# Order at the slot seams and both halves of the second MLP product beside the exponentials in a kernel of three transformer layers and a rotation

## The reference, cut to what matters

```
xn = ln(x) * (1 + sc1) + sh1                  # modulation from the condition
q, k, v = split(xn @ w_qkv + b_qkv)           # 16 heads of 18
q, k = ln(q), ln(k)                           # per head, layers 0 and 2 only
o = softmax(q @ k.T * 18**-0.5) @ v
x = x + g1 * (o @ w_proj + b_proj)
h = gelu((ln(x) * (1 + sc2) + sh2) @ w1 + b1) # 288 -> 1152
x = x + g2 * (h @ w2 + b2)                    # the second MLP product
```

## Time and profile before

| | us |
|---|---|
| median of 3 runs (lowest, highest) | 5283.6 (5277.15, 5285.2) |
| the profiled execution: its time | 5279.16 |
| its span in the trace | 5277.4 |
| PE busy | 4467.7 (85%) |
| DVE busy | 3683.8 (70%) |
| ACT busy | 2297.4 (44%) |
| POOL busy | 1110.9 (21%) |
| mean granted TensorE clock | 0.942 of full |

### The profile page before, as it was taken

The page is one execution under the profiler, slowest core; times in us unless marked ns, Lnnn a source line. Parts: engine busy times, 40 slices in busy tenths (PEclk is TensorE's granted clock), DMA queues, the critical chain, the costliest instruction groups (busy, mean ns, idle before and its releaser), DMA issues. The chain is left out here.

```text
span 5277.4 us, 125546 instructions
## 1 busy us (share of the span) xinstructions
PE 4467.7 (85%) x46073; PEld 3701.5 (70%) x46073; DVE 3683.8 (70%) x7723; ACT 2297.4 (44%) x3828; POOL 1110.9 (21%) x2044
## 2 busy tenths in 40 slices
PE   6654888888888886899999999976988989899888
PEld 4543677777777775777777777765777777777776
DVE  5665788777877774666666666656777777777774
ACT  0112445454444543444444444434444444444443
POOL 1001222222222212222222222212122121212121
PEclk7576999999999997999999999997999999999999
DMA  3001010010100001010000100011000000000000
GB/s 69 19 0 47 26 27 27 23 27 21 27 27 24 26 21 55 26 27 25 23 27 27 27 27 27 25 42 31 24 26 19 26 24 21 24 23 26 19 24 17
DMA packets 122230, 141.59 MB, mean 27 GB/s; under 512 B 14446, under 2 KB 117780, under 8 KB 122112
## 3 DMA queue, kind: packets, MB, share of 16 engines
q1 hardware_dynamic: 121968, 139.75, 9.7%
q10 hardware_dynamic: 144, 0.22, 0.0%
HBM read 110.87 MB, written 29.06 MB: 27 GB/s over the span
## 5 line engine op out<-in xcount | busy, mean ns | idle before, releaser
L627 ACT ACTIVATE pT<-S 128x1024 f32<-128x1024 f32 x768 | 745.2, 1022 | 467.5 <-PE S L1134 463.1
L863 DVE TENSOR_REDUCE mx<-S 128x4 f32<-128x1024 f32 x768 | 919.1, 1215 | 26.9 <-PE S L1105 20.0
L575 ACT ACTIVATE hf<-M 128x512 f32<-128x512 f32 (+1 forms) x480 | 266.8, 556 | 927.1 <-PE M L1185 842.7
L922 DVE TENSOR_TENSOR xbo<-M,gM 128x288 f32<-128x288 f32 x192 | 87.8, 457 | 784.1 <-PE M L1224 784.1
L1134 PE MATMUL S<-qT,kT 32*128 32x256 f32 x9216 | 432.2, 298 | 159.3 <-ACT nmT L614 83.7
L504 POOL TENSOR_SCALAR hh<-hf 128x512 fp32r<-128x512 f32 (+1 forms) x480 | 282.7, 589 | 1192.1 <-ACT hf L575 1173.5
L1134 PEld LDWEIGHTS S<-qT,kT 32*128 32x128 f32 x9216 | 336.3, 187 | 240.2 <-ACT pT L627 108.1
L1144 PE MATMUL A<-pT,V 128*32 128x256 f32 x6144 | 415.9, 389 | 19.6 <-ACT pT L627 19.6
L1185 PE MATMUL M<-xh,w_hi 128*128 128x256 f32 x1728 | 388.0, 304 | 4.6 <-POOL xh L480 3.3
L1185 PE MATMUL M<-xl,w_hi 128*128 128x256 f32 x1728 | 347.6, 284 | 40.4 <-DVE xm L786 40.4
L1105 PE MATMUL S<-kT,qT 32*128 32x256 f32 x3072 | 351.2, 337 | 30.9 <-DVE mx L863 24.0
(11 more groups left out here) (229 smaller groups left out, 10190.6 us busy)
## 6 DMA issues: line engine op xcount, KB each, us to landing
mid<-xbo SPq DMA_DIRECT2D x64, 288.0 KB, 3.2
xld<-mid SPq DMA_DIRECT2D x64, 288.0 KB, 3.0
xa<-mid SPq DMA_DIRECT2D x64, 288.0 KB, 3.5
gA<-gates SPq DMA_DIRECT2D x96, 144.0 KB, 3.3
gM<-gates SPq DMA_DIRECT2D x96, 144.0 KB, 3.0
xld<-in_x_dram SPq DMA_DIRECT2D x32, 288.0 KB, 3.5
xa<-in_x_dram SPq DMA_DIRECT2D x32, 288.0 KB, 3.5
out_dram<-xbo SPq DMA_DIRECT2D x32, 288.0 KB, 2.2
```

The source lines that it names most:

```text
L575: act.activation(hf[:, f % 2, 0:c], MBANK[f % 2][:, 0:c], ACT.Gelu if rot else ACT.Gelu_apprx_tanh).then_inc(s["m_hf"], 1)
L627: act.activation(pT[:, g % 2, 2 * h:2 * h + 2, :], S[:, 2 * h:2 * h + 2, :], ACT.Exp, scale=float(HD) ** -0.5).then_inc(s["a_ex"], 1)
L863: dve.tensor_reduce(mx[:, p, :, :], S[:, r:r + 2, :].rearrange("p a (t k) -> p a t k", t=NT), AX.X, ALU.max).then_inc(s["a_mx"], 1)
```

## The change

At the seam, the transposes of nm (`A_turn_max`) and their copy (`A_shift`) move from the head of the next slot to the end of the slot in which nm is made, between the q, k, v products 4 and 5. They go through bank 3 of S instead of ABANK[0], so the two waits on ABANK[0] pass to the first `A_pv`.

In layers 0 and 1 `down0` is issued one slot later, for sample d, beside the exponentials: 16 matmuls after the scores of group 0, 11 after the first `A_pv`; `down1` follows with 10 after the second `A_pv`, 12 and 5 after the scores of group 3. The transposes of `nxt`'s x move one group later, and ACT's reads of them too (after exponential 5 and 7 instead of 3 and 5). In layer 2 `down0` stays; `down1` is split 16 and 11 instead of 14 and 13.

On DVE, `M_x2` of half 0 goes from the head of the slot to behind `M_norm` (layer 2) or `A_heads_rstd` (layers 0 and 1), half 1 behind `A_heads_norm`; `A_xl` goes to behind the third maximum; `A_lo` goes behind `A_out`; `R_x3` ahead of both; the first `M_hl` ahead of the second maximum and behind `A_olo`. On PE `A_turn_n` goes ahead of the first two scores. On POOL the first two `M_hh` go ahead of `M_residual`. The diff, with one line of context and less indentation:

```diff
@@ -528,6 +528,8 @@
         if m is not None:
-            M_residual(m)
             if rot:
                 M_xh(m)
-            for f in range(5):
+            M_hh(m, 0)
+            M_hh(m, 1)
+            M_residual(m)
+            for f in range(2, 5):
                 M_hh(m, f)
@@ -613,3 +615,3 @@
         wait(act, "a_nmT", n, 1)
-        act.activation(nmT[:, :], ABANK[0][:, 0:T], ACT.Identity).then_inc(s["a_nmc"], 1)
+        act.activation(nmT[:, :], S[:, 3, 0:T], ACT.Identity).then_inc(s["a_nmc"], 1)
 
@@ -658,9 +660,8 @@
                 high_m(act, layer, range(KC))
-            A_shift(a)
             for i in range(2 * QUADS):
                 A_exp(a, p, i // 2, i % 2)
-                if nxt is not None and i == 3:
+                if nxt is not None and i == (3 if rot else 5):
                     A_xf(nxt, 0)
                     A_xf(nxt, 1)
-                if nxt is not None and i == 5:
+                if nxt is not None and i == (5 if rot else 7):
                     A_xf(nxt, 2)
@@ -710,2 +711,5 @@
             A_qkv(nxt, 4)
+        if p is not None:
+            A_shift(p)
+        if nxt is not None:
             A_qkv(nxt, 5)
@@ -944,4 +948,2 @@
             low_m_mix(dve, layer)
-        if d is not None:
-            M_x2(d, 0)
         if m is not None:
@@ -962,10 +964,12 @@
             M_norm(m)
+        if d is not None and rot:
+            M_x2(d, 0)
         if p is not None and eps is not None:
             A_heads_rstd(p)
-        if d is not None:
-            M_x2(d, 1)
+        if d is not None and not rot:
+            M_x2(d, 0)
         if p is not None and eps is not None:
             A_heads_norm(p, None)
-        if nxt is not None:
-            A_xl(nxt)
+        if d is not None:
+            M_x2(d, 1)
         if a is not None:
@@ -973,9 +977,6 @@
             A_oraw(a, 1)
-        if m is not None and not rot:
-            M_xl(m)
-        if p is not None:
-            A_lo(p, 0)
-            A_lo(p, 1)
         if d is not None and rot:
             R_x3(d)
+        if m is not None and not rot:
+            M_xl(m)
         if a is not None:
@@ -983,2 +984,4 @@
         if p is not None:
+            A_lo(p, 0)
+            A_lo(p, 1)
             A_max(p, 0)
@@ -986,6 +989,2 @@
             M_xl(m)
-        if p is not None:
-            A_max(p, 1)
-        if m is not None and not rot:
-            M_hl(m, 0)
         if a is not None:
@@ -993,4 +992,6 @@
         if m is not None:
-            if rot:
-                M_hl(m, 0)
+            M_hl(m, 0)
+        if p is not None:
+            A_max(p, 1)
+        if m is not None:
             M_hl(m, 1)
@@ -998,2 +999,4 @@
             A_max(p, 2)
+        if nxt is not None:
+            A_xl(nxt)
         if a is not None:
@@ -1108,10 +1111,7 @@
 
-    def A_turn_max(n, p):
+    def A_turn_max(n):
 
-        if p is not None:
-            wait(pe, "a_qkvd", p, 6)
-        wait(pe, "a_prd", n, 0)
         wait(pe, "a_nm", n, 1)
         for t in range(NT):
-            op = pe.transpose(ABANK[0][:, t * P:(t + 1) * P], nm4[:, t, :, :].rearrange("p r h -> p (r h)"), ident[:, :])
+            op = pe.transpose(S[:, 3, t * P:(t + 1) * P], nm4[:, t, :, :].rearrange("p r h -> p (r h)"), ident[:, :])
         op.then_inc(s["a_nmT"], 1)
@@ -1136,3 +1136,3 @@
 
-    def A_pv(n, g):
+    def A_pv(n, p, g):
 
@@ -1141,2 +1141,5 @@
             wait(pe, "a_v", n, 2)
+            wait(pe, "a_prd", n, 0)
+            if p is not None:
+                wait(pe, "a_qkvd", p, 6)
         for i in range(NT):
@@ -1260,4 +1263,5 @@
         def down0(lo, hi):
-            if m is not None:
-                M_down(m, 0, lo, hi)
+            n = m if rot else d
+            if n is not None:
+                M_down(n, 0, lo, hi)
 
@@ -1286,24 +1290,31 @@
         if a is None:
+            if not rot:
+                down0(0, 27)
             down1(0, 27)
         if a is not None:
-            A_turn_max(a, p)
             A_scoresT(a, 0)
-            down1(0, 14 if rot else 9)
+            (down1 if rot else down0)(0, 16)
             A_scoresT(a, 1)
-            A_pv(a, 0)
-            if rot:
-                down1(14, 27)
-        if nxt is not None:
+            A_pv(a, p, 0)
+            (down1 if rot else down0)(16, 27)
+        if nxt is not None and rot:
             A_turn(nxt, d, 0)
         if a is not None:
-            if not rot:
-                down1(9, 18)
             A_scoresT(a, 2)
-            A_pv(a, 1)
+            A_pv(a, p, 1)
+            if not rot:
+                down1(0, 10)
         if nxt is not None:
-            A_turn(nxt, d, 1)
-        if a is not None:
             if not rot:
-                down1(18, 27)
+                A_turn(nxt, d, 0)
+            else:
+                A_turn(nxt, d, 1)
+        if a is not None:
             A_scoresT(a, 3)
+            if not rot:
+                down1(10, 22)
+        if nxt is not None and not rot:
+            A_turn(nxt, d, 1)
+        if a is not None and not rot:
+            down1(22, 27)
         if rot and d is not None:
@@ -1311,3 +1322,3 @@
         if a is not None:
-            A_pv(a, 2)
+            A_pv(a, p, 2)
         if rot and d is not None:
@@ -1317,3 +1328,3 @@
         if a is not None:
-            A_pv(a, 3)
+            A_pv(a, p, 3)
         if rot and d is not None:
@@ -1332,6 +1343,6 @@
             first_up()
-        score(0)
-        score(1)
         if a is not None:
             A_turn_n(a)
+        score(0)
+        score(1)
         if rot:
@@ -1355,5 +1366,9 @@
         qkv(3)
-        down0(0, 14)
+        if rot:
+            down0(0, 14)
         qkv(4)
-        down0(14, 27)
+        if p is not None:
+            A_turn_max(p)
+        if rot:
+            down0(14, 27)
         qkv(5)
```

More of the change, by code:

```diff
@@ L962, in slot @@
                             M_norm(m)
+                        if d is not None and rot:
+                            M_x2(d, 0)
                         if p is not None and eps is not None:
                             A_heads_rstd(p)
+                        if d is not None and not rot:
+                            M_x2(d, 0)
+                        if p is not None and eps is not None:
+                            A_heads_norm(p, None)
                         if d is not None:
                             M_x2(d, 1)
-                        if p is not None and eps is not None:
-                            A_heads_norm(p, None)
-                        if nxt is not None:
-                            A_xl(nxt)
                         if a is not None:
@@ L973, in slot @@
                             A_oraw(a, 1)
+                        if d is not None and rot:
+                            R_x3(d)
                         if m is not None and not rot:
                             M_xl(m)
+                        if a is not None:
+                            A_out(a)
                         if p is not None:
@@ L978, in slot @@
                             A_lo(p, 1)
-                        if d is not None and rot:
-                            R_x3(d)
-                        if a is not None:
-                            A_out(a)
-                        if p is not None:
                             A_max(p, 0)
@@ L1286, in slot @@
                         if a is None:
+                            if not rot:
+                                down0(0, 27)
                             down1(0, 27)
                         if a is not None:
[L1289 removed]
                             A_scoresT(a, 0)
[L1291 removed]
+                            (down1 if rot else down0)(0, 16)
                             A_scoresT(a, 1)
[L1293 to L1296 removed]
+                            A_pv(a, p, 0)
+                            (down1 if rot else down0)(16, 27)
+                        if nxt is not None and rot:
                             A_turn(nxt, d, 0)
                         if a is not None:
+                            A_scoresT(a, 2)
+                            A_pv(a, p, 1)
                             if not rot:
[L1300 to L1302 removed]
+                                down1(0, 10)
                         if nxt is not None:
+                            if not rot:
+                                A_turn(nxt, d, 0)
+                            else:
+                                A_turn(nxt, d, 1)
+                        if a is not None:
+                            A_scoresT(a, 3)
+                            if not rot:
+                                down1(10, 22)
+                        if nxt is not None and not rot:
                             A_turn(nxt, d, 1)
[L1305 to L1308 removed]
+                        if a is not None and not rot:
+                            down1(22, 27)
                         if rot and d is not None:
@@ L1332, in slot @@
                             first_up()
+                        if a is not None:
```

(3 more changed lines are left out.)

3 lines of the change are left out of this document (removed).

## The result

| | before | after |
|---|---|---|
| median of the runs beside each other (lowest, highest), us | 5282.79 (5277.15, 5285.2) | 5570.55 (5537.25, 5575.67) |
| the profiled execution | 5279.16 | 5575.67 |
| ratio to before, 95% interval | | 1.0533 [1.0491, 1.0575] |
| mean granted TensorE clock | 0.942 | 0.873 |

The account below looks back on a forecast made before the run. PE was taken to set the pace, with small waits. 29 x (2.4 + 1.0 + 0.2) = 104 us off 5279.2 gave 5175, on the median 5179; stated forecast 5178 us, range 5090 to 5240.

Parts of the forecast that it names:

- The layout of the slot: Layer 1's new order on PE and DVE: A_x1 starts at 32.3, score 5 at 36.3, after PE waits 2.5 us.
- The seam: Head of each slot: moving nm's transposes and copy between q, k, v products 4 and 5 saves 1.6 us a slot.
- The slots: Slot lengths of layers 0, 1 and 2 after the change: 44.4, 44.1 and 51.1 us, 2.4, 1.0 and 0.2 less.
- Rival (3): Clock falls to 1.2 GHz at the 2.5 us wait before score 5: 3 us a slot more, 5439; chance 0.03.
- Two of my own signs: Listed as showing the forecast wrong: a clock under 0.95 in the steady slots, layer 2 above 51.5.
- the 2.8 us that are moved: Second MLP product beside the exponentials: of 3.6 us, 0.9 is covered by waits, 2.8 moved, not saved.
- 1.1 for A_xl: DVE's stretch from M_xl to A_x1: moving A_xl into it adds 1.1 us.
- gaining 0.2 a slot: Layer 2: the later score 5 costs 1.36 of the 1.6 us saved, leaving 0.2 less, 51.1 us.
- M_residual and the port: POOL's M_residual behind two M_hh frees M_xl, may delay the first M_hl: 0.3 us lost, bounds 0 and 1.51.
- The sum took 0.9 off: DVE from M_xl to A_x1: 0.9 us less, because only the copies of V still lie on POOL beside M_xl.
- The whole 1.51: Residual's full time on M_hl by the skill's rule alone: slots of layers 0 and 1 up to 1.2 us longer.

Follow-up runs that it names:

- run 2: The kernel before with only the seam moved (transposes of nm and their copy between q, k, v products 4 and 5), all layers: 5123.41 us, ratio 0.9707.
- run 1: The changed kernel plus 20 useless matmuls (14 in layer 2) in PE's wait ahead of score 5: 5283.84 us, ratio 1.0008.
- run 3: The changed kernel with only A_xl moved back on DVE, to right behind M_x2 of half 1: 5325.45 us, ratio 1.0081.
- run 6: The kernel before plus the seam, the second MLP product's move in layers 0 and 1 and M_x2's new place, other orders old: 5103.51 us, ratio 0.9661.
- run 5: The changed kernel with the second MLP product's matmuls and the transposes of x back in their old places: 5656.06 us, ratio 1.0717.
- run 11: Layers 0 and 1 exactly as in the changed kernel, layer 2 as before with only the seam moved: 5383.46 us, ratio 1.0195.
- run 8: The kernel before with the seam moved, plus R_x3 ahead of A_lo on DVE in layer 2: 5132.88 us, ratio 0.9723.

## Why the prediction was wrong, by its own steps

**The layout of the slot: right, close to the decimal.** With t from 2711.56: the last product with V starts at 17.21 (forecast 16.95), the transposes of the sums at 20.01 (19.8), M_xl at 19.15 (18.9), A_x1 at 32.81 (32.3), and PE waits 2.63 for the maximum (2.5). Score 5 starts at 37.15, not 36.3: more than half of that is A_x1's later start, the rest its longer additions and the maximum. The waits of 0.47 and 1.03 are gone; one of 0.61 for A_x1's x at product 0 was not foreseen.

**The seam: right.** 1.6 us a slot forecast; 1.56, 1.6 and 1.35 measured (run 2).

**The slots: too short, even had the clock held.** At 1.00 layers 0 and 1 have 45.14 and 44.75 (run 1) where I gave 44.4 and 44.1, 0.7 a slot too little. Layer 2 was further off. Its waits at the head were 1.05, 0.40 and 0.70 for the forecast 1.0, 0.6 and 0.8, and the 0.43 for M_xl's xm was missing; score 5 starts at t = 4643.51 - 4601.09 = 42.4, not 39.9. With the wait at score 5 filled its slots have 52.8 to 54.3 at a clock of 0.95 (run 1), and with A_xl out of the way 51.5 to 51.8 (run 3), against the forecast 51.1. So run 1, with the clock of layers 0 and 1 restored, took 5283.84 us, no less than the kernel before, and lies above the stated range as well: what layers 0 and 1 gain, 29 x (1.65 + 0.37) = 59, layer 2 loses again.

**The clock: the step that failed.** "Rival (3)" had the right mechanism and the right place, and its price of 3 us a slot was somewhat low: against run 1 the slots of layers 0 and 1 are longer by 3.5 and 4.1 on average (48.6 and 48.8 against 45.14 and 44.75), and its total of 5439 lies 131 below the measured one, for layer 2 averages 55.6. Together the slots explain the miss: 29 x (4.2 + 4.7 + 4.5) = 389 of 392. The rival got 0.03 because "PE is busy before and behind". That argument is what the runs refute: PE is busy 93% of the stretch, without a gap behind the wait, and yet the clock is 0.90 there. Two of my own signs ("a clock under 0.95 in the steady slots", "layer 2 above 51.5") are what came. The Trainium skill, page "TensorE: Matmul & The Clock Gate", section "HAM oscillation — how this bites in real kernels", states that idle gaps between bursts throttle the array again, and the runs agree. The kernel that the section describes waits longer between its bursts than the 2.6 us here, though, so the prediction's sentence that the rule "would make this rival the outcome" said more than the section does. What the rows left open deserved a larger chance than 0.03. The rows of before had no wait above about 1 us in the stretches at 1.00 and one of 1.81 in layer 2, so that 2.5 lay outside of all that the trace covered: what a trace does not cover is no evidence for "it holds".

**The order of DVE's work, not the MLP move, made the wait.** I blamed the wait on the 2.8 us that are moved and on 1.1 for A_xl together. Run 6 has the move and a wait of 0.17 at score 5; run 5 has no move and waits 2.6. Run 3 shows A_xl's share, 0.7. Which of the other moves in DVE's queue makes the remaining 1.9 was not tried one by one.

**Slower in the end also through layer 2** (some 165 of the 187 us of run 11), which I had gaining 0.2 a slot: its head has 2.6 us of waits within 6 us, a second place where the clock falls, which rival (3) did not have. That R_x3 ahead removes the wait of 1.81 is right, and what it is replaced by costs as much (run 8).

**M_residual and the port: the term was put together wrongly.** The sum took 0.9 off because only the copies of V would still lie beside M_xl. But in the kernel before M_xl ends at 2371.75 + 1.25 = 2373.00 and the residual's L496 begins at 2373.74; M_xl lay beside the copies of V and, from 2372.43 on, the first instruction of `M_residual`, L494. In the changed kernel it takes 1.25 too, beside the copies alone. What became shorter is only its second instruction (0.93 to 0.41). From M_xl to A_x1 DVE took 2744.37 - 2730.71 = 13.66 us, where I gave 13.4 to 13.5, so that other terms made up for it; that was luck. The first M_hl took 0.81 against 0.68. The whole 1.51, which by the Trainium skill's "SBUF — State Buffer", section "Who interferes with whom", could have fallen on M_hl, did not, but this slot does not test it: the residual (2738.20 to 2739.63) was nearly over when M_hl started at 2739.36. The 2.02 of M_xl beside `M_residual` in run 6 agree with the page in kind. The move was not undone alone, so its worth stays open.

Open as well is where exactly the cost begins. In the kernel before, layer 2 has a wait of 1.8 us in every slot (first fence, the waits over 600 us) and a clock of 0.99 (second), while the 1.92 of run 3 brought layers 0 and 1 to between 0.88 and 0.94:

```profile
PE M L1045 <- DVE xbo L930: 19.9, 11, 1.8
```

```profile
4200.00:4600.00 400.00, 359.92 (x3602) 293.27 (x3604) 300.76 (x632) 190.45 (x316) 80.68 (x153) 0.99 0.08 22
```

It is not the length of the wait alone: of two waits of 1.92 and 1.91 in run 3 only the second was followed by a low clock, and behind two waits of 2.63 in the changed kernel it was low for 3.5 us and for 13. What else decides was not tried.

## What to carry to other kernels

On a kernel that TensorE bounds, don't add up waits as if their length were their price: several waits of 0.2 to 1.1 us cost only themselves here, while one wait of 2.6 us cost another 3.5 to 4.1 us a slot, on average, in slower matmuls behind it. After a reordering, look at the granted clock of the steady stretches before anything else; if it fell, put independent matmuls into the longest wait, even useless ones, and that alone will tell what the clock took. Change the seam, the queue orders and the moved matmuls one at a time, since here one part gained 3% and another lost more than that.

## What was not expected of the hardware

- One wait of 2.6 us in a slot of 45 us, with PE busy 93% overall, lowered the granted clock from 1.00 to 0.90. A wait of 1.92 lowered it in some slots of run 3 and left it at 1.00 in others; four waits of 1.14 and less, 3.1 us in sum, did not lower it, and with one of 1.8 in layer 2 it was 0.99.
- Behind one and the same wait of 2.63 us the clock was low for 3.5 us in one slot and for 13 us in the slot before, at 0.50 with PE busy throughout.
- 14 matmuls a slot of no use in layers 0 and 1, with the two DVE instructions of A_xl moved, made a kernel 312 us faster (5383.46 to 5071.15); 20 and 14 of them alone, 287 us.
- With the clock low, a part that saves 156 us by itself (the seam) saved nothing: 5566.23 without it, 5570.55 with it, at a mean clock of 0.92 and 0.873.
